# Mixture-of-experts kernel on one core: a third streamed expert's low half moves to VectorE, four experts are split in a row in the first four slot tiles, and the gate products stand around the first transposes

## What is computed

```python
x = x + 0.5 * ffn(layernorm(x))        # mixture of experts, 8 experts, 2 chosen
x = x + attn(layernorm(x))             # gated recurrence, 6 heads of 128
x = x + 0.5 * ffn(layernorm(x))        # the same experts once more

def ffn(xf):
    top_scores, top_idx = top_k(xf @ gate_w.T + gate_b + bias, 2)
    gates = softmax(top_scores)
    h = silu(einsum('td,ehd->teh', xf, w1) + b1)      # H = 352
    y = einsum('teh,edh->ted', h, w2) + b2
    return sum over the 2 chosen experts of gate * y
```

## Time and profile before

| | |
|---|---|
| median of 3 runs | 836.29 us |
| their range | 833.68 to 837.17 us |
| the profiled execution | 835.22 us |
| its span in the profile | 833.4 us |
| TensorE busy | 766.6 us, 92% of the span |
| VectorE busy | 606.2 us, 73% |
| ScalarE busy | 360.4 us, 43% |
| mean granted clock of TensorE | 0.963 of full |

### The profile page before, as it was taken

The page is one execution under the profiler, slowest core; times in us unless marked ns, Lnnn a source line. Parts: engine busy times, 40 slices in busy tenths (PEclk is TensorE's granted clock), DMA queues, the critical chain, the costliest instruction groups (busy, mean ns, idle before and its releaser), DMA issues.

```text
span 833.4 us, 14109 instructions
## 1 busy us (share of the span) xinstructions
PE 766.6 (92%) x4222; PEld 424.2 (51%) x4223; DVE 606.2 (73%) x1014; ACT 360.4 (43%) x626; POOL 231.1 (28%) x226
## 2 busy tenths in 40 slices
PE   8599899999997997998999999999935999999998
PEld 5346465656563444444444444445513666666663
DVE  6885656666656669999989998896876555555557
ACT  5856334343433437446544654443261333333331
POOL 3212644445532001101210211102102444444431
PEclk9899999999997998899999999999976999999999
DMA  9984648975743701610451121265473573333698
GB/s 317 370 305 152 246 133 322 339 290 161 253 151 106 184 1 51 114 39 1 81 96 26 52 26 14 63 230 119 172 287 114 196 267 113 116 122 115 218 315 311
DMA packets 44955, 137.27 MB, mean 165 GB/s; under 512 B 5488, under 2 KB 5488, under 8 KB 41584
## 3 DMA queue, kind: packets, MB, share of 16 engines
q1 hardware_dynamic: 27536, 86.38, 29.1%
q0 software_dynamic: 17376, 50.34, 21.9%
HBM read 85.32 MB, written 51.38 MB: 164 GB/s over the span
## 4 chain that ended last, share of the span: by engine, by line
PE 76%; DVE 14%; ACT 3%; DMA 2%; issue 2%; POOL 2%; SPq 0%; DVEq 0%; ACTq 0%; POOLq 0%
PE bank L659 62%; PE bank L653 5%; PE bank L755 3%; PE bank L924 2%; PE bank L840 1%; DMA space<-xn_rows,slot_src 1%; DVE space L1414 1%; DVE space L1468 1%; DMA space<-x_in 1%; DVE space L1686 1%; POOL space L580 1%; DVE space L1683 1%; DVE bst L1405 1%; PE bank L858 1%; POOL rstd L612 1%
## 5 line engine op out<-in xcount | busy, mean ns | idle before, releaser
L659 PE MATMUL bank<-space 128*128 (+3 forms) x2894 | 577.9, 352 | 9.2 <-DVE space L1531 3.2
L659 PEld LDWEIGHTS bank<-space 128*128 128x128 f16 (+1 forms) x2894 | 274.3, 99 | 256.2 <-issue 24.3
L584 POOL DMA_INDIRECT y_rows<-space,slot_dst x78 | 86.2, 1105 | 157.3 <-DVE space L1539 156.7
L580 POOL DMA_INDIRECT space<-xn_rows,slot_src x78 | 81.7, 1047 | 117.9 <-PE bank L653 62.9
L1102 ACT ACTIVATE space<-bank 128x512 f16<-128x512 f32 x78 | 46.5, 596 | 140.8 <-PE bank L653 132.5
L1539 DVE TENSOR_SCALAR space<-bank,slot_gate 128x512 f32<-128x512 f32 x78 | 58.5, 751 | 60.3 <-PE bank L659 59.3
L1526 DVE SCALAR_TENSOR_TENSOR space<-bank,space 128x352 f32<-128x352 f32 x78 | 40.8, 524 | 59.2 <-PE bank L659 41.9
L1112 ACT ACTIVATE space<-bank 128x384 f16<-128x384 f32 x78 | 38.2, 489 | 94.6 <-PE bank L755 94.6
L1520 DVE TENSOR_TENSOR space<-bank,space 128x512 f16<-128x512 f32 x78 | 53.9, 691 | 32.4 <-ACT space L1102 30.4
L653 PE MATMUL bank<-ident,space 128*128 128x128 f32 x440 | 67.1, 283 | 10.3 <-DMA space<-xn_rows,slot_src 8.4
L1683 DVE SCALAR_TENSOR_TENSOR space<-space,cang 128x512 f32<-128x512 f32 x84 | 63.0, 750 | 5.4 <-ACT space L1194 3.2
(11 more groups left out here) (199 smaller groups left out, 751.1 us busy)
## 6 DMA issues: line engine op xcount, KB each, us to landing
space<-ffn_w SPq DMA_DIRECT2D x8, 1472.0 KB, 12.7
w_saved<-space SPq DMA_DIRECT2D x8, 1472.0 KB
space<-w_saved SPq DMA_DIRECT2D x8, 1472.0 KB, 9.0
xn_rows<-space SPq DMA_DIRECT2D x8, 1024.0 KB, 5.9
space<-y_rows SPq DMA_DIRECT2D x16, 512.0 KB, 5.0
space<-x_in SPq DMA_DIRECT2D x7, 1024.0 KB, 5.4
space<-att_w SPq DMA_DIRECT2D x12, 518.0 KB
space<-y_rows POOLq DMA_DIRECT2D x6, 1024.0 KB, 9.2
```

Of the source, the lines that this page charges most:

```text
L580: gp.indirect_dma_start(dst, None, rows, bass.IndirectOffsetOnAxis(ap=index, axis=0)).then_inc(done, 16)
L584: gp.indirect_dma_start(y_rows, bass.IndirectOffsetOnAxis(ap=slot_dst[:, t:t + 1], axis=0), yo[:, t % 2], None).then_inc(y_st[t % 2], 16)
L659: last = pe.matmul(dst, a, b, start=(n == 0), stop=(n == len(terms) - 1))
```

## The change

Expert 4 is no longer split through TensorE. `BYPE` becomes 2, so TensorE and ScalarE do 12 cuts rather than 18, the high half of expert 4 becomes one ScalarE instruction that stands ahead of all evictions of low pieces, and its low half goes to VectorE in step 0 of `slots(0)`, ahead of those of experts 5, 6 and 7. VectorE now does these four low halves in six cuts each (`low_cut`), and ScalarE the high halves of experts 5 to 7 in two parts each (`half_high`). Two of the low pieces move between the two groups of the one-hot products. The load of expert 6 also waits for the first transposes. In both phases the gate products are cut in two, one group before `xt(0)` and one behind it; VectorE computes `tile_exp` after `OHgate`, and the halves of the gates earlier; `ready` is computed (now in `marks`) after the first `x_low`; in phase 1 ScalarE computes the tanh between the normalised rows 5 and 6.

```diff
-BYPE = 3
+BYPE = 2
+HALVES = ((0, 3 * CH), (3 * CH, FW))
+LATER = OWN + BYPE
@@ SP
-                if OWN <= e - STAGES < OWN + BYPE:
+                if OWN <= e - STAGES < LATER:
                     sp.wait_ge(w_low, len(CUTS) * (e - STAGES - OWN + 1))
                 elif e >= STAGES:
-                    sp.wait_ge(w_ready, e - STAGES + 1)
+                    sp.wait_ge(w_ready, e - STAGES + 1 - (BYPE if e - STAGES >= LATER else 0))
+                if e == LATER + 2:
+                    sp.wait_ge(m_xt, 3)
@@ PE, low_piece and route
+                b = LOW_BANKS[n % (4 if n < AHEAD else 2)]
+                pe.wait_ge(w_hi, e - OWN + 1)
                 if n >= 4:
-                    pe.wait_ge(w_low, n - (3 if e < OWN + BYPE - 1 else 1))
+                    pe.wait_ge(w_low, n - (3 if n < AHEAD else 1))
                 for k in (0, 1):
+                    if k and not ph:
+                        for n in range(AHEAD, AHEAD + 2):
+                            low_piece(OWN + n // len(CUTS), n % len(CUTS))
                     pe.wait_ge(s_ohs, 2 * ph + k + 1)
@@ PE, slots
-                    for n in range(AHEAD, 2 * len(CUTS) + 4):
+                    for n in range(AHEAD + 2, BYPE * len(CUTS)):
                         low_piece(OWN + n // len(CUTS), n % len(CUTS))
                 pe.wait_ge(s_route, ph + 1)
+                slot_gates(ph, 0)
                 xt(0, 0, 0)
-                if not ph:
-                    for i in range(4, len(CUTS)):
-                        low_piece(OWN + BYPE - 1, i)
+                slot_gates(ph, 1)
+                pe.wait_ge(s_tiles, ph + 1)
                 pe.wait_ge(m_xl, o + 2)
                 up(0, 0, expert(0))
                 xt(1, 0, 1)
-                slot_gates(ph)
@@ ACT, before slots(0)
             split_high(OWN + 1)
-            for i in range(len(CUTS)):
-                low_piece(OWN, i)
...
-            for i in range(4):
-                low_piece(OWN + 2, i)
+            split_high(LATER)
+            for e in range(OWN, LATER):
+                for i in range(len(CUTS)):
+                    low_piece(e, i)
@@ ACT, steps of slots(0)
-                    if not ph and t < E - OWN - BYPE:
-                        split_high(OWN + BYPE + t)
+                    if not ph and t < E - LATER - 1:
+                        half_high(LATER + 1 + t, 0)
+                        half_high(LATER + 1 + t, 1)
@@ DVE
+            def low_cut(e, i):
+                at, w = CUTS[i]
+                v.wait_ge(w_hi, BYPE + 1 + (0 if e == LATER else 2 * (e - LATER) - (1 if at < HALVES[1][0] else 0)))
+                last = v.scalar_tensor_tensor(wexp[:, e, FW + at:FW + at + w], wstage[:, e % STAGES, at:at + w], WSCALE,
+                                              wexp[:, e, at:at + w], ALU.mult, ALU.subtract)
+                if i == len(CUTS) - 1:
+                    last.then_inc(w_ready, 1)
@@ DVE, steps of slots(0)
-                    if not ph and isinstance(t, int) and 1 <= t <= 3:
-                        split_low(OWN + BYPE + t - 1)
+                    if not ph and isinstance(t, int) and t < E - LATER:
+                        for i in range(len(CUTS)):
+                            low_cut(LATER + t, i)
```

More of the change, by code:

```diff
@@ L302, in build @@
         w_diff = sem("w_diff")
-        w_cut = sem("w_cut")
         w_low = sem("w_low")
@@ L322, in build @@
         s_rank = sem("s_rank")
+        s_tiles = sem("s_tiles")
         s_ohs = sem("s_ohs")
@@ L720, in route, with slot_gates @@
                 last.then_inc(s_inv, 1)
-            def slot_gates(ph):
-                pe.wait_ge(s_gates, ph + 1)
-                products(bank[5][:, KH * P:KH * P + SLOT_TILES],
-                         [(OHlo[ph][:, k, t, :], OHgate[ph][:, k, half * NT + t, 0:SLOT_TILES])
-                          for k in (0, 1) for half in (0, 1) for t in range(NT)]).then_inc(s_slotg, 1)
+            def slot_gates(ph, k):
+                pe.wait_ge(s_gates, 2 * ph + k + 1)
+                for n in range(2 * NT):
+                    last = pe.matmul(bank[5][:, KH * P:KH * P + SLOT_TILES], OHlo[ph][:, k, n % NT, :],
+                                     OHgate[ph][:, k, n, 0:SLOT_TILES], start=k + n == 0, stop=k == 1 and n == 2 * NT - 1)
+                if k:
+                    last.then_inc(s_slotg, 1)
             def slots(ph):
@@ L1352, in attention_end @@
                 for n in range(1, NT):
+                    if n == 6:
+                        act.wait_ge(s_dm, 2)
+                        act.activation(th, dm, ACT.Tanh, scale=0.5).then_inc(s_tanh, 1)
                     normalise_row(1, n)
@@ L1372, in _ @@
             split_high(OWN + 1)
-            for i in range(len(CUTS)):
-                low_piece(OWN, i)
-            for i in range(3):
-                low_piece(OWN + 1, i)
-            for i in range(3):
-                high_piece(OWN + 2, i)
-                low_piece(OWN + 1, i + 3)
-            for i in range(3, len(CUTS)):
-                high_piece(OWN + 2, i)
-            for i in range(4):
-                low_piece(OWN + 2, i)
+            split_high(LATER)
+            for e in range(OWN, LATER):
+                for i in range(len(CUTS)):
+                    low_piece(e, i)
             slots(0)
@@ L1451, in route @@
                                            ALU.add, ALU.mult))
+                v.wait_ge(s_tanh, ph + 1)
+                v.tensor_scalar(ghalf[:, 0], th, -0.25, 0.25, ALU.mult, ALU.add)
+                seq(v.tensor_scalar(ghalf[:, 1], th, 0.25, 0.25, ALU.mult, ALU.add))
+                ch(v.tensor_scalar(gscaled, ghalf[:, :, :], GSCALE, None, ALU.mult))
                 v.wait_ge(s_count, ph + 1)
@@ L1476, in route @@
                 ch(v.tensor_copy(SCL, counts[:, E - 2:E]))
-                seq(v.tensor_tensor(cmp, lane[:, 0:SLOT_TILES].unsqueeze(2).to_broadcast([P, SLOT_TILES, E]),
-                                    en.unsqueeze(1).to_broadcast([P, SLOT_TILES, E]), ALU.is_ge))
-                seq(v.reduce_sum(evf, cmp, AX))
-                seq(v.tensor_scalar(tile_exp[:, :], evf, float(E - 1), None, ALU.min))
                 v.wait_ge(s_inv, ph + 1)
@@ L1501, in route, with marks @@
                                                gpart[:, half, k].unsqueeze(2).to_broadcast([P, NT, SLOT_TILES]), ALU.mult)
-                        if k + half < 2:
+                        if not half:
                             ch(last)
-                last.then_inc(s_gates, 1)
+                    last.then_inc(s_gates, 1)
                 ch.wait()
+                seq(v.tensor_tensor(cmp, lane[:, 0:SLOT_TILES].unsqueeze(2).to_broadcast([P, SLOT_TILES, E]),
+                                    en.unsqueeze(1).to_broadcast([P, SLOT_TILES, E]), ALU.is_ge))
+                seq(v.reduce_sum(evf, cmp, AX))
+                v.tensor_scalar(tile_exp[:, :], evf, float(E - 1), None, ALU.min).then_inc(s_tiles, 1)
+                v.wait_ge(s_tiles, ph + 1)
+            def marks(ph):
                 seq(v.tensor_scalar(posf, SCL, 63.5, 1.0 / P, ALU.add, ALU.mult))
@@ L1561, in slots @@
                 x_low(0, 0)
+                marks(ph)
                 add_bias(0, 0)
```

26 lines of the change are left out of this document (6 added, 20 removed).

## The result

The changed kernel takes 840.28 us as a median of 20 runs (836.31 to 842.65), and the kernel before took 836.43 us beside it (20 runs, 833.68 to 839.25). The ratio is 1.0051, with a 95% interval of 1.0040 to 1.0062. It is slower, by 0.5%, where 0.1% faster was forecast. The profiled execution took 838.61 us with a span of 836.8 us, against 835.22 and 833.4 before: 3.4 us more.

What follows compares the result with a forecast made beforehand. TensorE, busy for 92% of the span, was taken as the bound, with waits where slots(ph) starts. 835.22 + 1.0 (phase 0) - 1.9 (phase 1) = 834.3; with 1.07 to the median, 835.3 us; range 831.0 to 840.5.

Steps and rivals of the forecast that it cites:

- TensorE's hole: Phase 0, after the fourth low piece: TensorE stands still for 4.05 us, 47.55 to 51.6, until the first eviction.
- `up(0)` starts, later by: Phase 0: up(0) starts at 66.8 us instead of 64.59, 2.2 us later than before.
- six cuts: Step 0 of phase 0: VectorE's six cuts for expert 4 take 3.5 us, at 0.61 us per cut.
- stores later by: End of the splits in phase 0: the last cut, and so the stores of w_saved, come about 3.7 us late.
- given back at tiles 7 and 8: Phase 0, behind the stores' start: tile 8's transposes come 10.2 us after it, not 12.96, giving back 2.7 us.
- phase 1 gives back: Phase 1, up to up(1): earlier slot_src and moved gate products gain 1.9 us, between 1.4 and 3.2 by the clock.
- the gathers in the stores: Phase 0: POOL's gathers get in between short cuts, tile 7's lands before the stores, and 2.7 us come back.
- (b): Rival: gathers stay shut out through back-to-back cuts, or stores hold the eighth tile; nothing comes back; +2.7, 838.0 us; chance 0.12.
- Rival (a): TensorE falls to half clock in its new phase 0 hole, slowing the pieces: +1.8, 837.1 us; chance 0.22.
- ScalarE's wait: Phase 0: ScalarE stands still from 41.3 to 48.2 us for expert 4's load; evictions start at 50.9, 6.5 us later.
- rival (c): VectorE's cuts cost more than 0.61 us; at 0.8 the 24 cuts cost 4.6 us more, 839.9 us; chance 0.1.
- Rival (d): No stall on ScalarE, as expert 4 lands by 41.3 us: 831.0 us; chance 0.16, together with an early clock in phase 1.

## Why the prediction was wrong

The measured ratio lies on the other side of 1 than forecast: 840.28 against 835.3.

| step | forecast | measured in the profile |
|---|---|---|
| third high half starts on ScalarE | 48.2 | 47.49 |
| first eviction | 50.9 | 50.05 |
| TensorE's hole | 4.05 | 2.75 |
| gather 0 | 60.7 | 59.77 |
| `up(0)` starts, later by | 2.2 | 1.5 |
| `up(1)` later by | 1.6 | 2.7 |
| six cuts | 3.5 | 3.56 |
| second split starts later by | 2.7 | 3.8 |
| each further split | 0.35 | 0.34 |
| stores later by | 3.7 | 4.8 |
| given back at tiles 7 and 8 | 2.7 | 0 |
| phase 1 gives back | 1.9 | 3.2, less 0.85 at tile 3 |

**The step that failed** is in the part on the gathers in the stores: "so it gets in at the end of the current instruction", and with it "that gives back 2.7". The measured value is 0. A POOL instruction that starts inside a row of cuts ends 0.84 to 0.86 us behind the last cut of the row, whatever its length and kind: behind one instruction of 3.21 us (99.52 against 98.67), behind six cuts (97.35 against 96.51), behind six `tensor_tensor` cuts (94.32 against 93.47), behind three cuts (86.97 against 86.11). One row speaks against it: in the kernel with the scatter between the cuts, the first of these scatters, at 73.46 us, took 1.20 and ended before its third cut did. I had taken four instructions of the earlier trace rows, whose operands and lengths are others, for the same thing, and had given the case in which the gathers stay shut out (b) 0.12. It came true as it was worked out, +2.7 us. With the scatter between the cuts the gathers were let in, and tile 8 came 9.81 us behind the stores in place of 12.96.

The Trainium skill (SBUF — State Buffer, section "Who interferes with whom") says that the loser of the shared pair is blocked for the whole instruction. The rows show more: it stays blocked through the next five as well.

**Mis-sized: the clock.** Rival (a) put +1.8 on a clock that falls in TensorE's hole, at 0.22. The profile of the change shows it at 1.00 through the hole and at 0.50 some 12 us later, for 1.6 us in `up(0)`. That is why `up(1)` is 2.7 and not 1.6 late. The profiles with a longer hole show it in the hole, as (a) had it. Held up by filling, the clock gives some 3.6 us of the median back (2.0 to 5.2 by both intervals), more than the 1.8 of the rival. The forecast had written down 839.8 for (a) and (b) together, near the end of its band. That this is close to the measured 840.28 is in part luck, as the sum below shows: in the profile the clock took 1.1 us, a wait at tile 3 that nobody forecast took 0.85, and phase 1 gave back 1.3 more than was put in.

The Trainium skill (TensorE: Matmul & The Clock Gate, section "Why this matters for your kernels") warns that idle gaps between bursts of matmuls bring the clock back to half, and would have made this rival the forecast. Three profiles agree, with holes of 3.78, 4.12 and 4.26 us and the clock at 0.50 behind them; in that of the change it was at 1.00 behind a hole of 2.75 us.

**Right.** ScalarE's wait was worked out to within 0.9 us, from one landing and three rows; the moved evictions and the one-hot groups follow as forecast, and so do the cuts, at 0.59 us each, so that rival (c) falls. Rival (d), no stall, did not occur by itself; made by hand it gave 0.9957.

**Phase 1** came out at its upper bound, 3.2 us, with the clock up by 640 us. It did not in every execution: of the other eleven kernels with these gate products, six have `up(0)` of phase 1 at 1.96 or 1.97 us in their profiles and five at 3.70, so the profile of the change was on the lucky side here. The wait of 0.75 us at tile 3 was not forecast. It stands beside the load of a saved expert at 642.75 us; that this is its cause is not shown.

**The sum.** The forecast's terms (835.22 + 1.0 - 1.9 + 1.07) add to 835.4, 0.1 above the figure given. In the profiled executions the difference to my sum of -0.9 is 4.3 us: 2.7 for the gathers, 1.1 for the clock in phase 0, 0.85 for tile 3, less 1.3 for a better phase 1; the last 0.9 or so I can't name from single rows (0.3 of it lies between tile 3 and TensorE's last products, most of the rest behind them).

## What to carry to other kernels

An instruction that waits for a transfer on an engine in order delays all that stands behind it: read from the landing when it can run, and put it behind the work that needs no transfer; here one line moved by twelve instructions was worth 0.94%. Where GpSimd has to get in beside VectorE, count a row of short VectorE instructions as one long one until a trace of those very operands says otherwise, and change the order so that GpSimd's instruction starts between rows. A hole in TensorE can cost more than its length: add the slower clock behind it, and expect that from run to run it is paid or not.

## What the runs showed of the hardware

- Six VectorE instructions of 0.6 us, back to back, hold a gather or a scatter of GpSimd until 0.85 us behind the last one (one scatter in a row of three got through in 1.20 us), while four `tensor_tensor` instructions of 0.74 us on f16 operands let a gather through in 1.22 us.
- Kernels that are alike up to there reach `up(0)` of a phase at either level of the clock (1.2 or 2.4 GHz), with 3.57 to 3.70 or 1.95 to 1.97 us for its 12 products. Once in phase 0 they took 3.63 us though TensorE had no idle time over 1.70 us between the first low piece and `up(0)`. With ScalarE's wait in place and nothing filled in, the hole in phase 0 was between 2.75 and 4.26 us long, as both of its ends move: the start of the third high half from 47.35 to 49.12 us, and the end of the fourth piece from 46.9 to 48.1.
- On SyncE's queue, a store of an expert issued right ahead of the load of the next attention piece made the pieces come 11 us apart, in place of 9.4 with the load ahead of the next store and 9.7 with the load ahead of the same number's store. The first cost 1.16% (1.0073 against 0.9957), more than the whole change.
